# A graph layer on one core: edge blocks of the rounds two to a segment, and four buffers for them

## The chip, the cores and the metric

The kernel runs on one core of one Trainium2 chip. The metric is the device time of one execution in microseconds (us). The profile is of one execution.

## The reference

The layer has N = 6250 nodes with 128 features, and E = 206250 edges with 128 features each, sorted by their target `dst`. What is computed:

```python
h = node_features @ W_node.T + b_node
e = edge_features @ W_edge.T + b_edge
msg = (h[src] + e) @ W_msg.T + b_msg
s = segment_sum(msg, dst)
deg = segment_sum(ones, dst)
out = layernorm(x + s / maximum(deg, 1)[:, None])
```

Since all of it up to the division is linear, the sum over a node's edges can be taken first, once of the edges' features and once of the x of their sources, and the weights applied after.

## The kernel before

Two streams of work are interleaved by a list of slots u = 0 to 135. Slots 0 to 10 (LEAD) are the lead. The 125 others are segments: 25 rounds (ROUNDS, one for each group of 250 nodes) of five segments s = 0 to 4 (SEGS). In the code g = u - LEAD counts segments, m is the round.

**Edge blocks.** The edges come in NS = 101 blocks t of 2048 (1 MB each). SP loads a block into one of EDGE_SLOTS = 3 buffers (`load_edges`, L365); a load waits until TensorE is through with the block that had the buffer (`l1_done`). VectorE makes a one-hot tile for each block (`make_onehot`, L683, ONEHOT_SLOTS = 3 buffers) and a placing matrix (`make_place`, L689, two buffers). TensorE sums the block into windows of 32 nodes (`sum_windows`, L513): 16 fp32 matmuls with 32 columns of weights, which the trace shows as 32 passes. ScalarE copies the windows out of PSUM (`copy_windows`, L1114), TensorE puts them in place (`place_windows`, L520), and VectorE adds the result to `sums_e` at a column that it reads into a register first (`add_sums`, L692 and L699).

**Segments.** Each segment has five fills. A fill is five matmuls that count, from one-hots of rows and keys, how often each source block occurs (`count_fill`, L565, three PSUM banks), and behind it 5 or 6 matmuls of 250 columns that apply the counts of the round before to x (`apply_counts`, L581). ScalarE moves each bank out (`move_bank`, L1167); fill k waits until bank k - 3 is moved. VectorE makes the one-hots for a whole segment ("hots", `make_hots`, L709, two buffers) one segment ahead: those for segment g + 1 may start once TensorE has filled the last bank of segment g - 1. In segment 1 of a round VectorE also makes the keys of the next round (`make_keys`, L723 to L738); TensorE turns them in segment 3 behind fill 2 (`turn_keys`), ScalarE spreads them (`spread_keys`, L1157).

**Finishing.** Group n is finished in segment 0 of round n + 2 on TensorE (`finish_group`, L597, behind fill 3), and in segment 1 on VectorE: message (L748), bias (L755), stats (L762), variance (L770), scale (L775, L777). ScalarE takes the root of the variance in segment 1 between moving banks 2 and 3 (`take_root`, L1179), and normalizes in segment 2 ahead of bank 0 (`normalize`, L1185). SP loads the residual (L384) and stores y (L388) at places in its own order of edge loads.

**Order.** In a segment each engine works in this order. TensorE: the block's sums, fill 0, fill 1, the block's placing, fills 2 to 4. ScalarE: the copy of the block, banks 0 to 4. VectorE: hots of the next segment, message, add_sums, bias, place, stats, one-hot, variance, scale, keys. Before the change a slot has one block or none (`block_at`): one in each slot of the lead, and 90 in segments 1 to 4 of the rounds, all but ten of these. Segment 0 has none.

**Lead.** Beside its 11 blocks the lead finds where each node's edges begin: a window of dst is gathered by POOL (L455), VectorE and ScalarE count in it (L803, L1127), the starts go to DRAM and back (L1132 to L1145), and small gathers fetch src (L463). x (3.2 MB) is loaded behind block 9. In rounds 0 and 1 VectorE also has checks and the splitting of x in three bf16 parts (L873, L879).

Of the kernel before, what the change touches and what calls it, by code (L numbers as in the profile page):

```python
# [27 lines left out]
SEGS = 5  # L28
# [4 lines left out]
G0 = 7  # L33
FIRST = 27
LEAD = 11
EDGE_SLOTS = 3
ONEHOT_SLOTS = 3
COUNT_BANKS = 3
BLOCK = 128
BELOW, ABOVE = 220, 358  # L40
# [4 lines left out]
def gnn_layer(nc, x, src, dst, edge_attr, w_node, b_node, w_edge, b_edge, w_msg, b_msg, out):  # L45
    N = x.shape[0]
    E = edge_attr.shape[0]
    NS = -(-E // SUP)
# [3 lines left out]
    ROUNDS = GROUPS  # L52
# [18 lines left out]
    SLOTS = LEAD + ROUNDS * SEGS  # L71
    group_of = [(G0 + m) % GROUPS for m in range(ROUNDS)]
    sup_of = [(FIRST + t) % NS for t in range(NS)]
    block_at, blocks_by = [], [0]
    for u in range(SLOTS):
        m, s = divmod(u - LEAD, SEGS)
        due = u + 1 if u < LEAD else LEAD + -(-(NS - LEAD) * (m * (SEGS - 1) + s) // (ROUNDS * (SEGS - 1)))
        block_at.append(blocks_by[-1] if due > blocks_by[-1] else None)
        blocks_by.append(due)
    slot_of = [block_at.index(t) for t in range(NS)]  # L80
    assert blocks_by[-1] == NS


    finish_slot = [LEAD + SEGS * (m + 2) if m < ROUNDS - 2 else SLOTS for m in range(ROUNDS)]
    finish_at = {u: m for m, u in enumerate(finish_slot) if u < SLOTS}
    summed_by = [blocks_by[u] for u in finish_slot]
    assert not any(block_at[u] is not None for u in finish_at)

    LIMIT_B = (42.5, 3.6)
    LIMIT_A = (7.3, 3.6)  # L90
# [6 lines left out]
    with ExitStack() as ctx:  # L97
# [385 lines left out]
        def _(pe):  # L483
# [117 lines left out]

            pe.wait_ge(rel_copied, 2)
            for u in range(SLOTS):
                t, g = block_at[u], u - LEAD
                if t is not None:
                    sum_windows(t)
                if u < LEAD:
                    if t == 1:
                        pe.wait_ge(count_taken, 1)
                        count_blocks(1)  # L610
                    if t == 4:
                        turn_weights()
                    if t == 8:
                        turn_slots(0)
                    place_windows(t)
                    if t == 5:
                        make_weights()
                    if t == 9:
                        turn_keys(0)
                    continue  # L620
                m, s = divmod(g, SEGS)
                for f in range(FILLS):
                    count_fill(g, f)
                    if m > 0:
                        apply_counts(m - 1, s * FILLS + f, ROUND_FILLS)
                    if f == 1 and t is not None:
                        place_windows(t)
                    if f == 2 and s == 3 and m + 1 < ROUNDS:
                        turn_keys(m + 1)
                    if f == 3 and u in finish_at:  # L630
                        finish_group(finish_at[u])
                    if f == 3 and g == 2:
                        turn_degrees()
                        turn_slots(1)
# [35 lines left out]
        def _(dve):  # L670
# [9 lines left out]
            def make_onehot(t):  # L680
                if t >= ONEHOT_SLOTS:
                    dve.wait_ge(l1_done, t - ONEHOT_SLOTS + 1)
                dve.tensor_tensor(onehot[:, t % ONEHOT_SLOTS, :, :], iota_bf[:, 0:W].rearrange("p (a w) -> p a w", a=1).to_broadcast([P, TILES, W]),  # L683
                                  rel_col[:, :, sup_of[t]:sup_of[t] + 1].to_broadcast([P, TILES, W]), ALU.is_equal).then_inc(onehot_ready, 1)
# [252 lines left out]
            make_onehot(0)  # L937
            make_place(0)
            make_onehot(1)
            block_counts(1)  # L940

            for u in range(SLOTS):
                t, g = block_at[u], u - LEAD
                n = finish_at.get(u - 1)
                if 0 <= g < SLOTS - LEAD - 1:
                    make_hots(g + 1)
                if n is not None:
                    add_message(n)
                if u < LEAD:
                    if t == 1:  # L950
                        begin_job(1)
                    if 2 <= t < 6:
                        count_nodes(0, [0, 3, 8, 13][t - 2], [3, 8, 13, 18][t - 2])
                    if t == 4:
                        dve.wait_ge(wm_turned, 1)
                        link(dve.tensor_copy(wm_t, x_ps[0][:, 0:D]))
                        dve.wait_ge(small_in, 96)
                        link(dve.tensor_scalar(bias_rep, ones[:, :], bias_col[:, 0:1], bias_col[:, 1:2], ALU.mult, ALU.add))
                        dve.sem_inc(wm_ready, 1)
                    if t == 5:  # L960
                        end_job(0)
                    if t == 6:
                        copy_weights()
                    if t == 7:
                        count_nodes(1, 0, JOB_DVE[1])
                    if t == 8:
                        end_job(1)
                        make_slots(0)
                    if t == 9:
                        make_keys(0)  # L970
                if t is not None:
                    add_sums(t)
                if n is not None:
                    add_bias(n)
                if t is not None and t + 1 < NS:
                    make_place(t + 1)
                if n is not None:
                    take_stats(n)
                if t is not None and t + 2 < NS:
                    make_onehot(t + 2)  # L980
                if n is not None:
                    take_variance(n)
                if u == LEAD - 1:
                    make_hots(0)
                if n is not None:
                    make_scale(n)
                if g >= 0:
                    m, s = divmod(g, SEGS)
                    if s == 1 and m + 1 < ROUNDS:
                        make_keys(m + 1)  # L990
                    if g == 0:
                        make_degrees()
                        check_order()
                    if g == 1:
                        check_sorted()
                    if g == 2:
                        make_slots(1)
                        check_slots()
                        copy_degrees()
                        for i in range(7):  # L1000
                            split_rest(i)
                    if g == 3:
                        for i in range(7):
                            split_low(i)
                        dve.sem_inc(early_done, 1)
                        dve.sem_inc(viol_ready, 1)
# [97 lines left out]
        def _(act):  # L1104
# [86 lines left out]
                act.copy(rel_col[:, k * 8:(k + 1) * 8, :], count_ps[k][:, :].bitcast(BF16).rearrange("p (t c) -> p t c", t=8)[:, :, 0:NS]).then_inc(rel_copied, 1)  # L1191
            roots, ends = 0, 0
            for u in range(SLOTS):
                t, g = block_at[u], u - LEAD
                if g >= 0 and g % SEGS == 0 and g // SEGS >= 2:
                    take_x(g // SEGS - 2)
                if t is not None:
                    copy_windows(t)
                if u < LEAD:
                    k0 = JOB_DVE[0]  # L1200
# [14 lines left out]
                m, s = divmod(g, SEGS)  # L1215
# [59 lines left out]
```

## Time and profile before

| | |
|---|---|
| median of 3 runs | 811.5 us (810.43 to 813.04) |
| the profiled execution | 810.29 us |
| its span, first to last instruction | 808.4 us |
| TensorE busy (matmuls) | 726.8 us, 90% |
| VectorE busy | 636.3 us, 79% |
| ScalarE busy | 461.0 us, 57% |
| GpSimd busy | 49.9 us, 6% |
| moved by DMA | 121.08 MB, 150 GB/s on average |
| chain that ended last | TensorE 85%, VectorE 7%, DMA 4% |

Busy time is the sum over the instructions of an engine. In the rows below L12 is line 12 of the kernel, PE is TensorE, PEld its weight loads, DVE is VectorE, ACT is ScalarE, POOL is GpSimd, and SP issues loads and stores. What stands in square brackets is the idle time of the engine just before the instruction and what ended it; "issue" is a wait for nothing that the profile shows.

### The profile page before, as it was taken

The numbers are of one execution on the slowest core, as the hardware profiler recorded it, in microseconds if no ns is written. First come the engines' busy times: TensorE is split into PE (matmuls) and PEld (weight loads), VectorE is DVE, ScalarE is ACT, GpSimd is POOL, SyncE is SP. The second block draws the span as 40 slices with busy tenths as digits, with TensorE's granted clock in tenths as the row PEclk, the third lists the DMA queues.
The fourth block names the chain that finished last, engine by engine and source line by source line (L and its number), as shares of the span: only waits on it lengthen the run. The fifth ranks groups of instructions, "written<-read, shape, count | busy, mean of one in ns | idle before, by whom it ended". The sixth has DMA issues, their size and how long they took to land.

```text
span 808.4 us, 24794 instructions
## 1 busy us (share of the span) xinstructions
PE 726.8 (90%) x10555; PEld 643.4 (80%) x10555; DVE 636.3 (79%) x1128; ACT 461.0 (57%) x938; POOL 49.9 (6%) x42
## 2 busy tenths in 40 slices
PE   3454636999999999999999999999999999999995
PEld 2333435988898899889889888988888988898895
DVE  6564998798789878888888888878887887788732
ACT  4343632666566566565656665666666656565641
POOL 2002100000000000000000000000000000000000
PEclk9655657999999999999999999999999999999998
DMA  7987431544535444544553465346334544454300
GB/s 223 248 266 232 154 106 54 167 135 155 163 122 177 161 151 138 174 130 137 186 174 119 127 208 168 97 140 221 122 124 156 173 156 128 165 169 134 99 15 15
DMA packets 71529, 121.08 MB, mean 150 GB/s; under 512 B 4486, under 2 KB 17502, under 8 KB 71315
## 3 DMA queue, kind: packets, MB, share of 16 engines
q1 hardware_dynamic: 68462, 115.72, 44.8%
q0 software_dynamic: 2336, 2.83, 1.3%
q8 instruction: 86, 1.41, 0.7%
q10 hardware_dynamic: 618, 0.90, 0.5%
q14 instruction: 27, 0.22, 0.1%
HBM read 116.18 MB, written 3.23 MB: 148 GB/s over the span
## 4 chain that ended last, share of the span: by engine, by line
PE 85%; DVE 7%; DMA 4%; issue 2%; ACT 1%; ACTq 0%; DVEq 0%; POOLq 0%
PE x_ps L581 49%; PE count_ps L565 18%; PE win_ps L513 12%; PE win_ps L520 3%; DMA edges<-in_edge_attr_dram 2%; PE misc_ps L597 1%; PE misc_ps L598 1%; DVE key_hot L709 1%; DVE x_rest L879 1%; DMA win_src<-in_src_dram,clipped_int 1%; DVE row_hot L803 1%; DMA region<-in_dst_dram 1%; DVE row_hot L709 1%; DVE x_rest L873 1%; DMA starts_dram<-edge_total 1%
## 5 line engine op out<-in xcount | busy, mean ns | idle before, releaser
L1167 ACT CAST region<-count_ps 128x490 bf16<-128x490 f32 x625 | 350.2, 574 | 174.1 <-PE count_ps L565 168.0
L581 PE MATMUL x_ps<-region,x_rest 128*128 128x250 bf16 x2450 | 449.3, 270 | 0.0
L581 PE MATMUL x_ps<-region,x_hi 128*128 128x250 bf16 x1225 | 332.6, 271 | 0.0
L709 DVE TENSOR_TENSOR row_hot<-iota_bf,row 125x3200 bf16<-125x3200 bf16 x125 | 227.8, 1822 | 94.6 <-PE count_ps L565 64.3
L565 PE MATMUL count_ps<-key_hot,row_hot 125*128 125x98 bf16 x3125 | 244.2, 209 | 28.3 <-DVE key_hot L709 28.2
L565 PEld LDWEIGHTS count_ps<-key_hot,row_hot 125*128 125x128 bf16 x3125 | 199.8, 99 | 57.0 <-DVE key_hot L709 29.9
L581 PEld LDWEIGHTS x_ps<-region,x_rest 128*128 128x128 bf16 x2450 | 229.6, 98 | 17.4
L709 DVE TENSOR_TENSOR key_hot<-iota_bf,key 125x2500 bf16<-125x2500 bf16 x125 | 181.7, 1454 | 0.0
L513 PE MATMUL win_ps<-edges,onehot 128*32 128x128 f32 x3232 | 118.7, 292 | 11.2 <-DMA edges<-in_edge_attr_dram 9.4
L581 PEld LDWEIGHTS x_ps<-region,x_hi 128*128 128x128 bf16 x1225 | 118.9, 97 | 8.0
L513 PEld LDWEIGHTS win_ps<-edges,onehot 128*32 128x32 f32 x3232 | 89.0, 116 | 32.6 <-issue 21.8
L463 POOL DMA_INDIRECT win_src<-in_src_dram,clipped_int x25 | 44.6, 1785 | 591.1 <-DVE key_bf L738 471.4
L1114 ACT COPY win_sb<-win_ps 128x128 f32<-128x128 f32 x101 | 26.9, 266 | 91.2 <-PE win_ps L513 81.7
L683 DVE TENSOR_TENSOR onehot<-iota_bf,rel_col 128x512 f32<-128x512 bf16 x101 | 68.8, 681 | 0.0
L520 PE MATMUL win_ps<-place,win_sb 128*128 128x128 f32 x202 | 43.9, 301 | 16.2 <-ACT win_sb L1114 13.8
L520 PEld LDWEIGHTS win_ps<-place,win_sb 128*128 128x128 f32 x202 | 32.7, 204 | 21.0 <-ACT win_sb L1114 18.3
L699 DVE TENSOR_TENSOR sums_e<-sums_e,win_ps 128x128 f32 x101 | 28.7, 284 | 15.9 <-PE win_ps L520 9.4
L689 DVE TENSOR_SCALAR place<-iota_f,pos 128x128 f32<-128x128 f32 x101 | 28.7, 284 | 0.1
L1179 ACT ACTIVATE stddev<-mean_var,eps_col 125x2 f32<-125x2 f32 x25 | 7.4, 296 | 35.0 <-DVE mean_var L770 35.0
L1185 ACT ACTIVATE y<-y,shift,rstd 125x128 f32<-125x128 f32 x50 | 22.0, 489 | 0.9 <-DVE shift L777 0.9
L748 DVE SCALAR_TENSOR_TENSOR y<-misc_ps,recip,resid 125x128 f32<-125x128 f32 x50 | 15.1, 343 | 8.9 <-PE misc_ps L598 8.9
L803 DVE TENSOR_SCALAR_CACHE_REDUCE row_hot<-region,job_node 125x578 bf16<-125x578 int32 (+7 forms) x25 | 17.0, 739 | 6.3 <-DMA region<-in_dst_dram,job_idx 6.3
(166 smaller groups left out, 318.6 us busy)
## 6 DMA issues: line engine op xcount, KB each, us to landing
edges<-in_edge_attr_dram SPq DMA_DIRECT2D x101, 1024.0 KB, 5.6
resid<-in_x_dram SPq DMA_DIRECT2D x25, 125.0 KB
out_dram<-y SPq DMA_DIRECT2D x25, 125.0 KB
region<-in_dst_dram ACTq DMA_DIRECT2D x1, 768.0 KB
win_src<-in_src_dram,clipped_int POOLq DMA_INDIRECT x25, 6.6
region<-in_L_gnn_W_node_dram SPq DMA_DIRECT2D x1, 64.0 KB
region<-in_L_gnn_W_edge_dram SPq DMA_DIRECT2D x1, 64.0 KB
region<-in_L_gnn_W_msg_dram SPq DMA_DIRECT2D x1, 64.0 KB
```

The lines of the kernel that those rows point to most:

```text
L463: pool.indirect_dma_start(out=win_src[:, m % 3, :], out_offset=None, in_=src.rearrange("(r e) -> r e", e=WE), in_offset=bass.IndirectOffse ...
L513: mm = pe.matmul(bank[q * W:(q + 1) * W, 0:D], hot[:, q * J + j, :], edges[:, t % EDGE_SLOTS, q * J + j, :], start=(j == 0), stop=(j == J ...
L520: pe.matmul(l2_ps[t % 2], win_sb[:, t % 2, :], place[:, t % 2, :], start=True, stop=True).then_inc(l2_done, 1)
L565: mm = pe.matmul(count_ps[fill % COUNT_BANKS][:, k * KEYS:(k + 1) * KEYS], row_hot[0:WE, g % 2, f * FILL + k, :], key_hot[0:WE, g % 2, f * ...
L581: mm = pe.matmul(x_ps[m % 2][:, 0:NB], rows, counts[m % 2][:, b, :], start=(n == 0), stop=(n == PARTS - 1))
L683: dve.tensor_tensor(onehot[:, t % ONEHOT_SLOTS, :, :], iota_bf[:, 0:W].rearrange("p (a w) -> p a w", a=1).to_broadcast([P, TILES, W]), rel ...
L689: dve.tensor_scalar(place[:, t % 2, :], iota_f[:, :], pos[:, sup_of[t]:sup_of[t] + 1], None, ALU.is_equal).then_inc(place_ready, 1)
L699: dve.tensor_tensor(to, to, l2_ps[t % 2], ALU.add).then_inc(added, 1)
L709: ins = dve.tensor_tensor(hot[0:WE, g % 2, :, :].rearrange("p w (a b) -> p w a b", b=4), iota_bf[0:WE, 0:width].rearrange("p (c a b) -> p ...
L803: dve.tensor_scalar(dve_junk[nodes[0] % 2][0:PB, 0:hi - lo], win_of[k][0:PB, lo:hi], job_node[k][:, i:i + 1], None, ALU.is_lt, ALU.add, ac ...
L1114: act.copy(win_sb[:, t % 2, :], win_ps[t % 2][:, 0:D]).then_inc(win_copied, 1)
L1167: act.copy(counts[m % 2][:, :, f * FILL * 2:(f + 1) * FILL * 2], count_ps[fill % COUNT_BANKS][:, 0:FILL * KEYS].rearrange("p (n b) -> p b ...
```

## The change

The blocks of the rounds are given out in pairs: 45 segments have two, the others none. `blocks_at` lists the blocks of each slot; the due time counts pairs. The lead keeps one block a slot. Edge buffers and one-hot buffers are four in place of three. TensorE sums both blocks at the segment's start and places both behind fill 1; ScalarE copies both at the start; VectorE adds both, then makes two places and up to two one-hots. Places and one-hots are counted by `placed` and `hot`: places run up to two ahead of the slot's last block, one-hots up to three ahead of its first.

```diff
-EDGE_SLOTS = 3
-ONEHOT_SLOTS = 3
+EDGE_SLOTS = 4
+ONEHOT_SLOTS = 4
...
-    block_at, blocks_by = [], [0]
+    blocks_at, blocks_by = [], [0]
     for u in range(SLOTS):
         m, s = divmod(u - LEAD, SEGS)
-        due = u + 1 if u < LEAD else LEAD + -(-(NS - LEAD) * (m * (SEGS - 1) + s) // (ROUNDS * (SEGS - 1)))
-        block_at.append(blocks_by[-1] if due > blocks_by[-1] else None)
+        pairs = -(-((NS - LEAD) // 2) * (m * (SEGS - 1) + s) // (ROUNDS * (SEGS - 1)))
+        due = u + 1 if u < LEAD else LEAD + 2 * pairs
+        blocks_at.append(list(range(blocks_by[-1], due)))
         blocks_by.append(due)
...
             for u in range(SLOTS):
-                t, g = block_at[u], u - LEAD
-                if t is not None:
+                g = u - LEAD
+                for t in blocks_at[u]:
                     sum_windows(t)
...
-                    if f == 1 and t is not None:
+                    for t in blocks_at[u] if f == 1 else []:
                         place_windows(t)
...
             make_onehot(1)
+            placed, hot = [1], [2]
             block_counts(1)
...
-                t, g = block_at[u], u - LEAD
+                ts, g = blocks_at[u], u - LEAD
+                t = ts[0] if ts else None
...
-                if t is not None:
+                for t in ts:
                     add_sums(t)
                 if n is not None:
                     add_bias(n)
-                if t is not None and t + 1 < NS:
-                    make_place(t + 1)
+                while ts and placed[0] < min(NS, ts[-1] + 1 + (1 if u < LEAD - 1 else 2)):
+                    make_place(placed[0])
+                    placed[0] += 1
                 if n is not None:
                     take_stats(n)
-                if t is not None and t + 2 < NS:
-                    make_onehot(t + 2)
+                while ts and hot[0] < min(NS, ts[0] + ONEHOT_SLOTS):
+                    make_onehot(hot[0])
+                    hot[0] += 1
...
-                if t is not None:
+                for t in blocks_at[u]:
                     copy_windows(t)
```

## Rows read from the trace of the kernel before

**Rows 1.** Table of stretches: busy us (instructions) by engine, clock, DMA share, GB/s.
```profile
160.00:780.00 620.00, 620.00 (x9222) 554.78 (x9220) 512.12 (x833) 387.39 (x788) 35.56 (x19) 1.00 0.46 148
```

**Rows 2.** Waits of the run: who for whom, us in total, times, longest.
```profile
PE count_ps L565 <- DVE key_hot L709: 28.2, 5, 9.5
...
PE win_ps L513 <- DMA edges<-in_edge_attr_dram: 9.4, 2, 9.1
```

**Rows 3.** The waits of TensorE's weight loads from 160 us on.
```profile
PEld win_ps L513 <- issue: 16.9, 82, 0.2
```

**Rows 4.** Timeline, TensorE at a block: start us, us, engine, line [idle before].
```profile
406.43 0.27 PE L581 MATMUL x_ps<-region,x_rest 128*128 128x250 bf16 x1
...
406.63 1.08 PE L513 MATMUL win_ps<-edges,onehot 128*32 128x128 f32 x32
407.64 0.25 PEld L565 LDWEIGHTS count_ps<-key_hot,row_hot 125*128 125x128 bf16 x5 [0.20 <-issue]
```

**Rows 5.** Chain that ended last, a fill and a placing: start us, us, what.
```profile
136.78 0.22 PE count_ps L565 x5
137.00 0.64 PE x_ps L581 x6
137.65 0.23 PE win_ps L520 x2
```

**Rows 6.** The timeline, the sum behind that placing.
```profile
138.01 0.29 DVE L699 TENSOR_TENSOR sums_e<-sums_e,win_ps 128x128 f32 x1 [0.63 <-PE win_ps L520]
```

**Rows 7.** Timeline, VectorE in the finishing segment that begins at 406.54.
```profile
409.92 0.29 DVE L699 TENSOR_TENSOR sums_e<-sums_e,win_ps 128x128 f32 x1
...
410.65 0.28 DVE L689 TENSOR_SCALAR place<-iota_f,pos 128x128 f32<-128x128 f32 x1
...
411.24 0.68 DVE L683 TENSOR_TENSOR onehot<-iota_bf,rel_col 128x512 f32<-128x512 bf16 x1
411.83 0.24 DVE L770 BATCH_NORM_AGGREGATE mean_var<-stats 125x2 f32<-125x6 f32 x2
...
414.04 1.82 DVE L709 TENSOR_TENSOR row_hot<-iota_bf,row 125x3200 bf16<-125x3200 bf16 x1
```

**Rows 8.** Timeline, VectorE in the lead: a sum and the instruction ahead.
```profile
76.19 0.29 DVE L738 SCALAR_TENSOR_TENSOR key_bf<-past,src_block 125x125 bf16<-125x125 bf16 x1
77.00 0.29 DVE L699 TENSOR_TENSOR sums_e<-sums_e,win_ps 128x128 f32 x1 [0.52 <-issue]
```

**Rows 9.** The timeline, ScalarE's casts and TensorE's fill 1 of the next segment.
```profile
410.04 0.57 ACT L1167 CAST region<-count_ps 128x490 bf16<-128x490 f32 x1 [0.52 <-PE count_ps L565]
...
412.31 1.02 ACT L1167 CAST region<-count_ps 128x490 bf16<-128x490 f32 x2
...
414.10 0.39 PE L565 MATMUL count_ps<-key_hot,row_hot 125*128 125x98 bf16 x5
```

**Rows 10.** Timeline, round 0: from a segment's one-hots to its first count.
```profile
113.13 1.81 DVE L709 TENSOR_TENSOR row_hot<-iota_bf,row 125x3200 bf16<-125x3200 bf16 x1
...
116.37 0.83 PE L565 MATMUL count_ps<-key_hot,row_hot 125*128 125x98 bf16 x8 [9.50 <-DVE key_hot L709]
```

**Rows 11.** The table of stretches, 2 us each, in the lead.
```profile
16.00:18.00 2.00, 1.22 (x24) 1.25 (x28) 2.00 (x4) 0.00 (x0) 0.00 (x0) 1.00 0.31 54
24.00:26.00 2.00, 0.46 (x2) 0.30 (x2) 1.07 (x3) 0.00 (x0) 1.20 (x1) 1.00 1.08 230
```

**Rows 12.** The chain that ended last, the load of block 3.
```profile
18.76 15.29 DMA edges<-in_edge_attr_dram
```

**Rows 13.** The timeline, VectorE's sums of block 3.
```profile
37.43 0.29 DVE L699 TENSOR_TENSOR sums_e<-sums_e,win_ps 128x128 f32 x1
```

**Rows 14.** Gathers of dst (L455): duration ns, first and last start us, landing.
```profile
L455 POOL DMA_INDIRECT region<-in_dst_dram,job_idx x2: 1196/1324/1452, 14.2 to 24.2; - x2
...
DMA to landing us min/median/max: 12.9/15.0/17.1
```

**Rows 15.** The small gathers of src (L463) up to 100 us: landing.
```profile
DMA to landing us min/median/max: 3.1/5.8/7.1
```

More of the change, by code:

```diff
@@ L73, in gnn_layer @@
     sup_of = [(FIRST + t) % NS for t in range(NS)]
-    block_at, blocks_by = [], [0]
+    blocks_at, blocks_by = [], [0]
     for u in range(SLOTS):
         m, s = divmod(u - LEAD, SEGS)
-        due = u + 1 if u < LEAD else LEAD + -(-(NS - LEAD) * (m * (SEGS - 1) + s) // (ROUNDS * (SEGS - 1)))
-        block_at.append(blocks_by[-1] if due > blocks_by[-1] else None)
+        pairs = -(-((NS - LEAD) // 2) * (m * (SEGS - 1) + s) // (ROUNDS * (SEGS - 1)))
+        due = u + 1 if u < LEAD else LEAD + 2 * pairs
+        blocks_at.append(list(range(blocks_by[-1], due)))
         blocks_by.append(due)
-    slot_of = [block_at.index(t) for t in range(NS)]
-    assert blocks_by[-1] == NS
+    slot_of = [next(u for u in range(SLOTS) if t in blocks_at[u]) for t in range(NS)]
+    assert blocks_by[-1] == NS and max(len(ts) for ts in blocks_at) <= 2
     finish_slot = [LEAD + SEGS * (m + 2) if m < ROUNDS - 2 else SLOTS for m in range(ROUNDS)]
@@ L86, in gnn_layer @@
     summed_by = [blocks_by[u] for u in finish_slot]
-    assert not any(block_at[u] is not None for u in finish_at)
+    assert not any(blocks_at[u] for u in finish_at)
     LIMIT_B = (42.5, 3.6)
@@ L1193, in _ @@
             for u in range(SLOTS):
-                t, g = block_at[u], u - LEAD
+                g = u - LEAD
                 if g >= 0 and g % SEGS == 0 and g // SEGS >= 2:
                     take_x(g // SEGS - 2)
-                if t is not None:
+                for t in blocks_at[u]:
                     copy_windows(t)
```

## The prediction

> **What bounds the kernel now.** I read the table of stretches first. From 160 to 780 us TensorE is busy in every microsecond at full clock, VectorE for 512 of the 620 and ScalarE for 387 [rows 1]. So in the rounds each microsecond of TensorE's queue is one of the kernel's, and the other two engines have room on average, though perhaps not at every place. The waits of the whole run come next. TensorE's long ones, 28.2 us in five for one-hots of VectorE and 9.1 us once for an edge block [rows 2], all lie in the lead and in round 0, where VectorE splits x. Then the weight loads from 160 us on: they never wait for an engine worth the name, but 82 times for "issue" ahead of L513, 16.9 us in all [rows 3], and as much again behind each block ahead of L565 [rows 4]. That is once on either side of every edge block, and it is what the change can halve. Last I read one finishing segment instruction by instruction, to see how late VectorE and ScalarE may be there.
>
> **Part 1, the blocks on TensorE: a saving.** Last matmul of a fill at 406.43, next due 0.11 later (six take 0.64 us [rows 5]), so segment 1 of this round begins at T = 406.54. The first L513 starts at 406.63, 0.09 late. The 32 passes take 1.08 us and the last lasts 0.27 us like the wide one ahead of it [rows 4], so they start (1.08 - 0.27) / 31 = 0.026 us apart and the 33rd would start at 407.46. The first L565 starts at 407.64, 0.18 late [rows 4]. A block alone costs 1.10 us, of which 0.27 is the two borders; a second block right behind costs 0.83 if the border between two equal shapes is free. I take it as free, since the four waits ahead of it (one-hots, copy, sums, edges) are all on things long done. Saving: 45 pairs x 0.27 = 12.15 us. If only the border behind the block is saved: 45 x 0.18 = 8.1; if a second block pays all that a first pays, nothing. The placing matmuls L520 take 0.23 us each [rows 5], run between full-width ones and have no such border: 202 before and after, no change.
>
> The Trainium skill (TensorEngine Tiling (Array Packing), Tiling Modes, Key Properties) says "Changing tiling mode (not just tile) drains the TensorE". Its page TensorE: Matmul & The Clock Gate, Part 2, puts the drain at about 128 cycles, 0.053 us at 2.4 GHz, so two borders would be 0.11 us and 45 of them an estimated 4.8 us in place of 12.15. The rows show 0.09 and 0.18; the duration in the trace goes before the page's figure.
>
> **Part 2, the finishing segment on VectorE: a cost.** Counting the new schedule out, pairs fall on segments (1,3), (1,3), (1,4), (2,4), (2) of five rounds, five times over. Group n is finished in segment 1 of rounds 2 to 24, so a pair meets the finishing in 13 rounds: 8 of the kind (1,3) and 5 of the kind (1,4). VectorE's order there is: one-hots of the next segment, message (L748), sums of the blocks (L699), bias, places, stats, one-hots of the blocks, variance (L770), scale, keys, then the hots of the segment after. All times now from T [rows 7]. Before: sums at 3.38, variance ready at 5.53 (L770 starts at 411.83, two in 0.24), next hots at 7.50.
> With the pair:
> - The first placing comes after both blocks and two fills of 0.87 us (136.78 to 137.65 [rows 5]): 1.93 + 1.74 + 0.23 = 3.90. A sum follows its placing by 0.13 us (L520 from 137.65 for 0.23 [rows 5], L699 at 138.01, which waited for it [rows 6]): 4.03. That is 0.65 later than 3.38.
> - The second sum reads its column offset into a register first. Where VectorE's sequencer can't run ahead of the sum, this shows: L738 issued at 76.19 and L699 at 77.00, 0.81 us [rows 8]. Here the sequencer stands at the wait of the first sum until 4.03, so it can't read ahead: +0.81. The near bound is a sum's own 0.29 plus some 0.05 for its semaphore: +0.34. I take 0.81, as the row is of the same instruction in the same position.
> - A second place: it and two stats take 0.59 (410.65 to 411.24), a third of that is 0.19. A second one-hot takes 0.59 (411.24 to 411.83) [rows 7].
> Sum 0.65 + 0.81 + 0.19 + 0.59 = 2.24 us (bounds 1.77 and 2.3).
>
> **Who waits for that.** ScalarE takes the root of the variance between moving bank 2 and bank 3 of this segment. Before, it cast bank 3 at 412.31, 0.24 behind the variance, and 0.57 later (a cast alone, 410.04), at T + 6.34, the bank was free; TensorE wants it for fill 1 of the next segment, at 414.10 = T + 7.56 [rows 9]. Slack 1.22. With the pair in segment 1 and none in segment 2 TensorE comes there at 1.93 + 0.46 + 4.28 + 0.87 = 7.54 (a segment without a block is five times 0.22 and 29.4 matmuls of 0.108, or 4.28) and the bank is free at 6.34 + 2.24 = 8.58. TensorE stands still for 1.04 us, in 13 rounds: 13.5 us.
> Then the hots of segment 3. From the start of row_hot to the first L565 that uses it 3.24 us pass (113.13 to 116.37 [rows 10]), so they are there at 7.50 + 2.24 + 3.24 = 12.98. TensorE leaves segment 2 at 6.67 + 4.28 + 1.04 = 11.99. In the kind (1,3) it has 1.93 us of blocks to do first: no wait, 0.9 us to spare. In the kind (1,4) it has none: 0.99 us more, 5 times, 5.0 us. Together 18.5 us. With the near bound of the second sum the first stall is 0.57 and the second unchanged: 7.4 + 5.0 = 12.4. Above, some 0.1 us a round for the normalizing that ScalarE has also to do: 20.
> Elsewhere VectorE has time: in segments 3 and 4 it runs ahead and its sums wait for nothing, so the second costs 0.34, and a pair 2.2 us in a segment of 6.67. The next hots (of segment 0) wait for the keys, as before, and come 0.7 us ahead of TensorE in the round with one pair, the tightest.
>
> **Part 3, round 0 and the lead: small, uncertain.** In round 0 VectorE is the bound [rows 2]. Ahead of the hots that release round 1 it now makes one more sum and two more places (the one-hots are as many; the extra one of the lead lies in an idle stretch): 0.2 + 2 x 0.19 = +0.6 us.
> The fourth buffer lets load 3 leave right behind the small loads; before, it left at 18.76 and landed at 34.05 [rows 12]. The DMA engines were 0.31 busy from 16 to 18 us and 1.08 from 24 to 26 [rows 11]. TensorE's 9.1 us there go. But VectorE, counting, comes to the sums of that block only at 37.43, and then waits for nothing [rows 13], so this gain I cost at nothing. The counting itself starts when the window of dst lands, 17.1 us after its issue at 14.2 [rows 14]. That window (124 rows of 1650 words, 0.82 MB) had the engines nearly to itself from 16 to 20 us, at 54 GB/s and more: 0.3 MB. The other 0.52 MB took the 11.3 us to 31.3, 46 GB/s. With load 3 beside it those 0.3 MB take 6.5 us in place of 4: 2.5 us later, and all behind it with it. Bounds 0 and +3. Load of x and blocks 10 to 12 also leave a block earlier, so the first small gather of src (68 us) meets a shorter queue; such gathers landed in 3.1 to 7.1 us [rows 15]. I take 1.0 off, bounds 0 and 4.0. Together +1.5, between -4 and +3.
> SP's queue: x, the residuals and the stores stand behind a load that is released a block earlier. A store behind the second load of a pair waits for its y until some 10 us into the round, and delays an edge load that has 15 us left. Nothing.
>
> **The sum.** -12.15 + 18.5 + 0.6 + 1.5 = +8.5 us. The profiled execution took 810.3 us (span 808.4 and 1.9 around it), the median of the three runs is 811.5. So 818.8 by the one and 820.0 by the other; I say 819.
>
> **The rivals.**
> A, VectorE's lateness is covered (faster). On average VectorE has room, 108 of 620 us [rows 1]. If the variance comes less than 1.22 us later (that is the point at which it decides, at the first L770 of a paired segment 1), only the borders count: 810.3 - 12.15 + 2.1 = 800.3. Against it: 0.65 + 0.19 + 0.59 alone, with a second sum for nothing, is 1.43. Chance 0.15.
> B, the second sum is cheap (0.34): -12.15 + 12.4 + 2.1 = +2.4, 812.7. Against it stands the 0.81 of [rows 8]. Chance 0.15, half of it within the bound of no change.
> C, the change doesn't do what it says: the second block pays its borders too. TensorE then comes 0.27 later to the bank, the stalls are 13 x 0.77 + 5.0 = 15.0, and with 2.1 that is +17.1, 827. Against it: five matmuls of one shape in a row show no border anywhere, only L513's neighbours do [rows 3, 4]. Chance 0.12, which also covers that only a part of the 0.27 is saved.
> By the Trainium skill's figure of the drain, above, the time would be an estimated 826, next to C.
> Forecast: 0.58.
>
> **How the numbers follow.** The forecast's own range goes from 814 (lead -4) to 824 (8.1 us of saving, stalls of 20). The range of 8 in 10 takes in B and C and leaves A out: 806 to 828, the low end being B with the lead's best. About 0.3% (2.4 us) is what a measurement of this kernel can tell from no change. Faster by more: A and the low end of B, 0.17. Within: 0.10. Slower: 0.73.
>
> **What would show it.** Right: issue waits ahead of L513's loads from 160 us on down from 82 to about 41; a second L513 block 0.83 us behind the first; about 13 waits of TensorE or its weight loads at the count for ScalarE's cast, 1 us each, and 5 for key_hot; VectorE idle 0.5 us between two sums in segment 1. Wrong: no waits of TensorE after 160 us (A), or issue waits still 82 or more (C). The lead shows in when the window lands (31.3 before).

## The result and the profile after

The kernel with the change takes 830.16 us (median of four runs, 829.68 to 831.59). The kernel before, beside it on the same chip, takes 810.96 (810.39 to 813.04). The ratio is 1.0218, with a 95% interval of 1.0186 to 1.0249: slower by some 19 us. The forecast was 819.0 with a range of 806 to 828, so the result lies outside it. The sign was as forecast, and so was the mechanism in the rounds; the size was under half, +8 us where +19 came, and the lead lost by a path that the forecast did not have. The profiled executions span 808.4 us before and 827.9 us after, 19.5 us more; the rest of the text accounts for these 19.5.

First the waits of TensorE's weight loads and matmuls from 160 us on, in the kernel after. The columns are: who waited at which line, for whom, us in total, times, longest.

```profile
PEld count_ps L566 <- ACT region L1172: 19.1, 13, 1.8
PEld win_ps L514 <- issue: 8.4, 41, 0.2
PEld count_ps L566 <- issue: 8.1, 41, 0.2
PEld count_ps L566 <- DVE key_hot L710: 5.3, 6, 1.0
```
```profile
PE count_ps L566 <- ACT region L1172: 15.5, 13, 1.5
PE count_ps L566 <- DVE key_hot L710: 3.6, 5, 0.7
```

The issue waits ahead of L514 (L513 before) went from 82 to 41 [rows 3]. Thirteen waits for ScalarE's cast and five for key_hot are new, in exactly the numbers counted out of the schedule. The table of stretches shows the same from TensorE's side. The columns are us, then busy us (instructions) of PE, PEld, DVE, ACT and POOL, the clock, the DMA share and GB/s.

```profile
160.00:780.00 620.00, 600.88 (x9028) 547.06 (x9026) 511.85 (x818) 376.82 (x775) 35.54 (x19) 1.00 0.44 146
```

TensorE was busy in all of the 620 us [rows 1]; now it is idle for 19.1, which is the 15.5 and 3.6 of its own waits above. VectorE's busy time is unchanged, 512 us.

The finishing segment answers [rows 4], [rows 7] and [rows 9]. Here is the timeline of the same segment of the same round. TensorE's two blocks and the count behind them come first, then the last matmul of fill 0 of the segment after, and the late count of fill 1:

```profile
418.54 0.27 PE L582 MATMUL x_ps<-region,x_rest 128*128 128x250 bf16 x1
418.74 1.95 PE L514 MATMUL win_ps<-edges,onehot 128*32 128x128 f32 x64
420.62 0.40 PE L566 MATMUL count_ps<-key_hot,row_hot 125*128 125x98 bf16 x5
...
426.07 0.27 PE L582 MATMUL x_ps<-region,x_hi 128*128 128x250 bf16 x1
427.51 0.40 PE L566 MATMUL count_ps<-key_hot,row_hot 125*128 125x98 bf16 x5 [1.17 <-ACT region L1172]
```

VectorE and ScalarE in between:

```profile
422.90 0.29 DVE L700 TENSOR_TENSOR sums_e<-sums_e,win_ps 128x128 f32 x1 [0.98 <-PE win_ps L521]
423.72 0.29 DVE L700 TENSOR_TENSOR sums_e<-sums_e,win_ps 128x128 f32 x1 [0.53 <-DVE sums_e L700]
423.92 0.61 DVE L756 SCALAR_TENSOR_TENSOR y<-bias_row,has_edge,y 125x128 f32<-125x128 f32 x2
424.44 0.48 DVE L690 TENSOR_SCALAR place<-iota_f,pos 128x128 f32<-128x128 f32 x2
...
425.24 1.27 DVE L684 TENSOR_TENSOR onehot<-iota_bf,rel_col 128x512 f32<-128x512 bf16 x2
426.43 0.24 DVE L771 BATCH_NORM_AGGREGATE mean_var<-stats 125x2 f32<-125x6 f32 x2
```
```profile
426.70 0.29 ACT L1184 ACTIVATE stddev<-mean_var,eps_col 125x2 f32<-125x2 f32 x1 [2.89 <-DVE mean_var L771]
426.90 1.02 ACT L1172 CAST region<-count_ps 128x490 bf16<-128x490 f32 x2
```

The segment begins at T = 418.65 (418.54 and 0.11). The first sum is at T + 4.25, the second 0.82 later, the variance starts at T + 7.78 (before: 411.83 - 406.54 = 5.29 [rows 7]). ScalarE stands 2.89 us at the root with a filled bank behind it. TensorE was due to go on at 426.18 (426.07 and 0.11, T + 7.53) and does so at 427.51: 1.33 us of stall. (The row says 1.17 idle, as it counts the matmul ahead as busy for 0.27 us and not for 0.11; the 0.16 have to be added to each idle time to get the stall.) Twelve of the thirteen are like this one. The other, at 317.19, is 1.67 us, where the second sum came 1.17 behind the first.

Five times TensorE also waits for the hots, at the first count of segment 3 in the kind (1,4). The first of the five:

```profile
181.56 0.27 PE L582 MATMUL x_ps<-region,x_hi 128*128 128x250 bf16 x1
182.55 0.40 PE L566 MATMUL count_ps<-key_hot,row_hot 125*128 125x98 bf16 x5 [0.71 <-DVE key_hot L710]
```

It was due at 181.67 (181.56 and 0.11) and is 0.88 us late, as are the four others. The stalls are thus 12 x 1.33 + 1.67 = 17.6 us and 5 x 0.88 = 4.4 us.

In the lead, two things moved. VectorE's first count of the dst window, which began at 31.34 before:

```profile
34.75 0.58 DVE L804 TENSOR_SCALAR_CACHE_REDUCE row_hot<-region,job_node 125x358 bf16<-125x358 int32 x1 [9.62 <-DMA region<-in_dst_dram,job_idx]
```

And the write of the starts to HBM (L1139), whose completion lets ScalarE fetch them back (L1145), after and then before:

```profile
52.89 0.32 ACTq L1139 DMA_DIRECT2D starts_dram<-edge_total  x1
61.29 0.27 ACTq L1145 DMA_DIRECT2D region<-starts_dram  x1
```
```profile
49.57 0.39 ACTq L1134 DMA_DIRECT2D starts_dram<-edge_total  x1
54.61 0.27 ACTq L1140 DMA_DIRECT2D region<-starts_dram  x1
```

Issue to fetch is 8.4 us after and 5.0 before. What lies between is x: its load leaves SP's queue at 45.36 after and at 49.72 before, so after, the write goes out into its traffic.

```profile
45.36 0.87 SPq L379 DMA_DIRECT2D x_rest<-in_x_dram  x1
46.27 11.28 SPq L380 DMA_DIRECT2D x_rest<-in_x_dram  x1
```
```profile
49.72 0.86 SPq L378 DMA_DIRECT2D x_rest<-in_x_dram  x1
```

The table of stretches at the write, before and then after, has the DMA engines 0.02 busy (8 GB/s) and 1.06 busy (293 GB/s):

```profile
48.00:50.00 2.00, 1.07 (x21) 0.58 (x12) 1.66 (x12) 0.00 (x0) 0.00 (x0) 0.50 0.02 8
```
```profile
52.00:54.00 2.00, 0.08 (x4) 0.00 (x0) 1.01 (x10) 0.00 (x0) 0.00 (x0) 1.00 1.06 293
```

To split the run into lead and rounds I use two landmarks that exist in every version: the sixth row_hot, which releases round 1 (124.57 before, 132.23 after), and the rest of the span behind it (683.8 and 695.7). So of the 19.5 us, 7.7 are in the lead and round 0, and 11.9 in the rounds. Over the seven profiles of kernels with single blocks the rest is 682.7 to 684.1 us, so a difference of a few us in it is clear. The split has one weakness: VectorE has added three blocks of round 0 at the landmark before, four after, and two with pairs in segments 2 and 4, so some 1 us may stand on the wrong side of it.

### The profile page after: what moved, and what is told of

Same layout as the page of the kernel before. It is cut to its first block, busy times and chain, and to the rows that moved or that the text cites. A ratio compares the mean times of both kernels' runs of the same rounds, so it can differ in the third digit from the quotient of the medians.

```text
span 827.9 us, 24794 instructions
## 1 busy us (share of the span) xinstructions
PE 718.7 (87%) x10555; PEld 646.8 (78%) x10555; DVE 642.0 (78%) x1128; ACT 456.8 (55%) x938; POOL 49.9 (6%) x42
## 4 chain that ended last, share of the span: by engine, by line
PE 72%; DVE 16%; DMA 5%; issue 3%; ACT 2%; DVEq 1%; ACTq 0%; POOLq 0%
PE x_ps L582 42%; PE count_ps L566 15%; PE win_ps L514 10%; DMA region<-in_dst_dram,job_idx 3%; DVE onehot L684 2%; PE win_ps L521 2%; DVE row_hot L710 2%; DVE key_hot L710 2%; PE misc_ps L598 1%; PE misc_ps L599 1%; DVE sums_e L700 1%; DVE row_hot L804 1%; DMA starts_dram<-edge_total 1%; DVE y L756 1%; DVE x_rest L880 1%
## 5 line engine op out<-in xcount | busy, mean ns | idle before, releaser
L514 PE MATMUL win_ps<-edges,onehot 128*32 128x128 f32 x3232 | 111.0, 293 | 1.8 <-issue 1.8
L514 PEld LDWEIGHTS win_ps<-edges,onehot 128*32 128x32 f32 x3232 | 93.0, 118 | 14.6 <-issue 12.6
L684 DVE TENSOR_TENSOR onehot<-iota_bf,rel_col 128x512 f32<-128x512 bf16 x101 | 65.4, 683 | 0.0
L521 PE MATMUL win_ps<-place,win_sb 128*128 128x128 f32 x202 | 35.8, 298 | 32.4 <-ACT win_sb L1119 26.7
L521 PEld LDWEIGHTS win_ps<-place,win_sb 128*128 128x128 f32 x202 | 28.8, 202 | 36.4 <-ACT win_sb L1119 30.6
L690 DVE TENSOR_SCALAR place<-iota_f,pos 128x128 f32<-128x128 f32 x101 | 25.0, 285 | 0.0
```

The costliest lines, as they stand in the source:

```text
L514: mm = pe.matmul(bank[q * W:(q + 1) * W, 0:D], hot[:, q * J + j, :], edges[:, t % EDGE_SLOTS, q * J + j, :], start=(j == 0), stop=(j == J ...
L521: pe.matmul(l2_ps[t % 2], win_sb[:, t % 2, :], place[:, t % 2, :], start=True, stop=True).then_inc(l2_done, 1)
L690: dve.tensor_scalar(place[:, t % 2, :], iota_f[:, :], pos[:, sup_of[t]:sup_of[t] + 1], None, ALU.is_equal).then_inc(place_ready, 1)
```

## The experiments

Two theories stand at the start. One is the prediction's: the rounds lose because the pairs that fall on segment 1 delay the variance, and this has nothing to do with the buffer; the lead loses by the buffer. The rival is that the pairs themselves, or the fourth buffer's traffic, make the rounds slower everywhere.

Every kernel below computes the whole output. "Before" and "after" are the two kernels; ratios are to the kernel before, measured beside each. "Lead" is the time of the sixth row_hot, "rest" the span behind it.

**The buffer alone.** The kernel before with

```diff
-EDGE_SLOTS = 3
+EDGE_SLOTS = 4
```

> The kernel before with a fourth edge buffer and nothing else. Theory (two places: the buffer costs the lead, the pairs cost the rounds): the window of dst lands some 3.4 us later and the starts come back some 3.3 us later, as in the changed kernel; 810.3 + 6.7 = 817. Rival (the rounds carry all 19.5 us, the lead's shift has another cause in the schedule): 810 to 811.

816.88 us against 813.53, ratio 1.0047 (1.003 to 1.0065). Lead 132.82, rest 682.8. The rounds are untouched (683.8 before), and the whole cost is in the lead: VectorE starts counting at 37.05 and the starts take 8.6 us from write to fetch (55.20 to 63.76). The wait of 9.1 us for load 3 [rows 2] is gone, and nothing came of it. The 817 expected was met in the number only: it was 810.3 and 6.7, and the kernel before took 813.53 here, so the buffer cost 3.4 us by the medians, half of that. The profiled execution of the kernel before, with 810.3, had the shortest gather of dst of all with three buffers and no load held for it, as the table at the end of this section shows.

**The pairs alone.** The kernel after with `EDGE_SLOTS = 3` (its one-hot buffers stay at four).

> The changed kernel with three edge buffers; one-hots stay at four. Theory: the lead is that of before, the rounds those of the changed kernel (13 bank stalls of 1.3 us, 5 hots stalls of 1 us, borders -10.3): 830.2 - 6.7 = 823.5. Rival: 830. If instead the pairs need the fourth buffer, TensorE waits for edges in the rounds and it is over 830.

825.06 us, ratio 1.016 (1.0129 to 1.0191). Lead 126.23, rest 695.3 (after: 695.7). The row of waits for the cast is that of the kernel after to the digit, and so is the one for key_hot:

```profile
PEld count_ps L566 <- ACT region L1172: 19.1, 13, 1.8
...
PEld count_ps L566 <- DVE key_hot L710: 5.3, 6, 1.0
```

So buffer and pairs act in different places: the pairs cost the rounds 11.5 us, the buffer costs the lead. Their timed costs, 1.6% and 0.5%, add up to the 2.2% of the change within the intervals.

**Pairs away from the finishing segment.** The kernel of the pairs alone, with its pairs only in segments 2 and 4 of a round:

```diff
-        pairs = -(-((NS - LEAD) // 2) * (m * (SEGS - 1) + s) // (ROUNDS * (SEGS - 1)))
+        pairs = -(-((NS - LEAD) // 2) * (m * 2 + s // 2) // (ROUNDS * 2))
```

> The run with three edge buffers, but the 45 pairs on segments 2 and 4 alone, so that none meets the finishing in segment 1. Theory (the collision is the rounds' whole cost): no waits of TensorE for casts or hots after 160 us, 823.5 - 22.4 = 801, which is 10 us under the kernel before (the borders). Rival (a pair itself is dear wherever it stands, since VectorE and ScalarE are late behind every pair): 815 to 823.

800.89 us (800.05 to 801.66), ratio 0.9852 (0.9829 to 0.9875). Lead 125.40, rest 672.8: 11.0 us less than before. This is the run that decides. It has as many pairs, as many second sums and as many doubled places as the one above and takes 24 us less (825.06 and 800.89), so a pair is not dear in itself; it is dear in the finishing segment. The 801 expected, and no waits for casts or hots but the one that was there before, were met. The waits from 160 us on and the stretch:

```profile
PEld win_ps L514 <- issue: 8.4, 41, 0.2
PEld count_ps L566 <- issue: 8.1, 41, 0.2
...
PEld count_ps L566 <- DVE key_hot L710: 0.3, 1, 0.3
```
```profile
160.00:780.00 620.00, 619.94 (x9315) 569.34 (x9313) 520.10 (x837) 387.02 (x791) 35.53 (x19) 1.00 0.44 148
```

TensorE is busy throughout again, and does more in the same 620 us: 9315 matmuls and not 9222.

**The root behind the last bank.** The pairs alone, with ScalarE's root behind bank 4 of the finishing segment and its normalizing behind bank 1 of the next:

```diff
-                if u - 2 in finish_at:
-                    normalize(ends)
-                    ends += 1
...
-                    if f == 2 and u - 1 in finish_at:
+                    if f == 1 and u - 2 in finish_at:
+                        normalize(ends)
+                        ends += 1
+                    if f == 4 and u - 1 in finish_at:
```

> The run with three edge buffers and pairs as in the change, but ScalarE takes the root behind bank 4 of segment 1 and normalizes behind bank 1 of segment 2, so that no bank stands behind the variance. Theory (the bank is what TensorE waits for first, the hots of segment 3 second): the 13 cast waits go, the hots waits grow as TensorE comes 1.3 us sooner, 5 x 2.3 + 8 x 0.3 = 13.9 in place of 22.4 us, so 815. Rival (VectorE's lateness alone is the cost and the order on ScalarE doesn't matter): 823.5.

819.18 us (815.69 to 821.57), ratio 1.0063 (1.0041 to 1.0086). The rest is 688.4, 6.9 less than with the pairs alone. The waits for the cast are gone, and those for the hots have grown:

```profile
PEld count_ps L566 <- DVE key_hot L710: 16.3, 14, 2.7
```

That shows the first stall's chain: with the root out of the casts' way the same late variance costs TensorE nothing at the bank. But TensorE then comes 1.3 us sooner to the hots of segment 3, which are as late as before, and waits there, one segment on:

```profile
PE count_ps L566 <- DVE key_hot L710: 12.5, 13, 2.4
```

In the five rounds of the kind (1,4) the idle time there is 2.1 to 2.4 us where it was 0.7, and the eight others are small (at most 0.6). TensorE's idle time from 160 us on goes from 19.1 us (15.5 and 3.6, as in the kernel after) to 12.5. The expectation had this pattern, and 8.5 us less in all; the rest is 6.9 less, the medians 5.9. The 6.9 us are a third of the 22.5 by which the rest exceeds that with no pairs in the finishing segment (695.3 and 672.8).

**The column offsets read ahead.** The pairs alone, with the offsets of both sums read into registers ahead of the first sum:

```diff
-                for t in ts:
-                    add_sums(t)
+                for t, at in zip(ts, [sums_at(t) for t in ts]):
+                    add_sums(t, at)
```

> Pairs as in the change, three edge buffers, but VectorE reads the column offsets of both sums ahead of the first sum. Theory (the 0.82 us between the two sums is the register read behind a wait): the second sum follows 0.35 us behind the first, the 13 cast stalls shrink by 0.47 us each to 0.86, the hots stalls stay as both sides move alike: -6.1 us against the run with three edge buffers (ratio to the kernel before 1.016 there, 1.008 to 1.009 here). Rival (the gap is the second sum's wait for the first one's result): no change, 1.016.

823.15 us against 812.59, ratio 1.0148 (1.0115 to 1.018). Lead 130.58, rest 690.6, 4.7 less than with the pairs alone (the lead of this execution was late by its gather, see below). VectorE in the same round, and TensorE's wait:

```profile
418.74 0.29 DVE L702 TENSOR_TENSOR sums_e<-sums_e,win_ps 128x128 f32 x1 [0.98 <-PE win_ps L521]
419.24 0.29 DVE L702 TENSOR_TENSOR sums_e<-sums_e,win_ps 128x128 f32 x1 [0.21 <-DVE sums_e L702]
```
```profile
PEld count_ps L566 <- ACT region L1174: 14.5, 13, 1.1
```

The second sum is 0.50 us behind the first in place of 0.82. So the register read behind the wait is 0.32 us of it; the sum's own 0.29 and an idle 0.21 for its wait on the sum ahead remain. 13 x 0.32 = 4.2 us follows for the stalls, and 4.6 are measured (19.1 to 14.5). The expectation was 0.35 us between the sums and 6.1 us less: it took the whole gap but the sum itself for the register read, and the wait for the first sum, which it had as the rival, is a part of it too. The timed ratios of the two kernels, 1.0148 and 1.016, can't be told apart by their intervals; the gain is read from the rest and the waits.

**Load of x later.** The kernel with four buffers, and x loaded behind block 10 and not block 9:

```diff
-                if t == 9:
+                if t == 10:
                     load_x()
```

> The kernel before with four edge buffers, but x loaded behind block 10 instead of block 9, so that it leaves after about the same block's sums as before. Theory (x in flight makes the write of the starts late): the write lands 5.0 to 5.5 us behind its issue in place of 8.6, the window of dst lands as late as with four buffers: some 3 us less than with four buffers alone. Rival (the greater depth of edge loads does it): 8 us and more, the time stays.

815.63 us, ratio 1.0042 (1.0026 to 1.0059). Lead 130.34, rest 684.1. The write of the starts now goes out just ahead of x (54.83), and its fetch follows in 5.3 us, as in the kernel before:

```profile
54.79 0.32 ACTq L1134 DMA_DIRECT2D starts_dram<-edge_total  x1
60.07 0.27 ACTq L1140 DMA_DIRECT2D region<-starts_dram  x1
```

So the load of x is the cause of the slow write. Of the 3.3 us that this gives back the lead keeps 2.5 (132.82 to 130.34): VectorE began counting 0.4 us earlier here (36.65 and 37.05), and its wait for the first small gather of src is 1.2 us longer (6.0 and 4.8). The timed ratio moves by 0.0005 only, less than its interval, where some 3 us less were expected: the write's cost is read from the traces, and no timing shows it.

**Load 3 held.** The kernel with four buffers, in which load 3 waits until block 0 is summed, as with three buffers:

```diff
+                elif t == 3:
+                    sp.wait_ge(l1_done, 1)
```

> The kernel before with four edge buffers, but load 3 held until block 0 is summed, as with three. Theory (load 3 beside the gather of dst makes that late): the gather lands about 17 us behind its issue as before, at most 1 us more since load 4 now leaves with load 3; the write of the starts still takes 8.6 us; some 3 us less than with four buffers alone. Rival (the loads behind block 3 do it): the gather takes 21 us or more as with four buffers.

815.45 us, ratio 1.0035 (1.002 to 1.0049). Lead 131.54, rest 683.7. The write of the starts took 8.35 us, as expected with x early. But the gather of dst took 21.5 us and not the 17 that this hold should have brought back, and the time is not clear of that of four buffers alone (1.0047). Here loads 3 and 4 leave together once block 0 is summed, so the edge loads beside the gather are still one more than with three buffers.

**Four buffers, pairs away from the finishing segment.** The kernel after, with only the line of the pairs changed as above.

> The changed kernel with four edge buffers and one line altered: the pairs on segments 2 and 4 alone. Theory: the rounds lose their 22 us of stalls, the lead keeps its 4 to 6 us: ratio to the kernel before 0.985 (as measured with three buffers) + 0.005 to 0.008 = 0.990 to 0.993, near 805. Rival (four buffers are what hurts the pairs): more than that of three buffers by over 1%.

806.03 us (805.43 to 807.0), ratio 0.9929 (0.9904 to 0.9954). Lead 131.26, rest 673.2. The gather took 21.8 us, the starts 8.4. One line of the schedule is worth 0.029 of the time to the kernel after, some 23 us, and by the ratios the fourth buffer costs this version 0.008 against the one with three (0.9852), some 6 us.

**The gather first.** The version with three buffers and pairs in segments 2 and 4, in which SP sends load 3 only when the first dst window has landed:

```diff
+                if t == EDGE_SLOTS:
+                    sp.wait_ge(job_win_in[0], 16)
```

> Three edge buffers, pairs on segments 2 and 4, and SP holds load 3 (and so all behind it) until the first gather of dst has landed. Theory (edge loads beside the gather make it late): alone from 16 us on it moves 54 to 96 GB/s and lands 11 to 15 us behind its issue in place of 17 to 22; block 3 comes late, but VectorE counts meanwhile; 3 to 5 us less than without the hold (ratio to the kernel before 0.985 there, 0.979 to 0.981 here). Rival (the gather is slow by itself): it lands at 17 us or more and the time stays or grows, as the edges come late.

800.78 us against 813.19, ratio 0.9849 (0.9807 to 0.9891): the time of the version without the hold (0.9852), where 3 to 5 us less were expected. Alone, the window lands 13.3 us after its issue and VectorE starts at 27.52, idle only 1.00; but now TensorE stands for block 3:

```profile
27.52 0.59 DVE L806 TENSOR_SCALAR_CACHE_REDUCE row_hot<-region,job_node 125x358 bf16<-125x358 int32 x1 [1.00 <-DMA region<-in_dst_dram,job_idx]
```
```profile
36.60 1.94 PE L516 MATMUL win_ps<-edges,onehot 128*32 128x128 f32 x32 [9.34 <-DMA edges<-in_edge_attr_dram]
```

VectorE has counted by then, and waits for the sum of that block:

```profile
39.85 0.29 DVE L702 TENSOR_TENSOR sums_e<-sums_e,win_ps 128x128 f32 x1 [6.24 <-PE win_ps L523]
```

It began 5.0 us earlier than without the hold (27.52 and 32.49) and stands 6.24 us here; the starts go out at 51.68 us and not at 50.50. That edge loads beside the gather make it late is shown; that its lateness alone costs the run is not.

**The spread of the lead.** The kernel before twice more, and the kernel with four buffers once more:

> The kernel before once more, for the spread of its lead. Theory (with three buffers the gather of dst lands 17 to 22 us behind its issue from run to run, with four always 21 to 23): a landing in 17 to 22, the write of the starts back after 5.0 to 5.7 us. Rival (the gather's time is the buffers' alone): 17.1 again.

> The kernel before a third time: as for the second look, gather in 17 to 22 us, starts in 5.0 to 5.7 us.

> The kernel before with four edge buffers once more. Theory: the gather lands 21 to 23 us behind its issue, the write of the starts is back after 8.3 to 8.7 us. Rival (both vary at random): values down to 17 and 5.

| | us | gather of dst | write to fetch of starts | lead |
|---|---|---|---|---|
| before again | 813.08 | 20.6 | 5.3 | 128.26 |
| before, third | 809.77 | 17.8 | 5.3 | 125.18 |
| four buffers again | 819.37 | 21.7 | 8.6 | 133.39 |

The gather of the kernel before thus took 17.1 us [rows 14] to 20.6, and its lead came out up to 3.7 us apart (124.57 to 128.26). With three buffers it took 17.1, 17.4, 18.4, 21.1, 21.9, 20.6 and 17.8 us (mean 19.2), with four 21.1, 22.7, 22.5, 21.5 (load 3 held), 21.8 and 21.7 (mean 21.9). By the means the fourth buffer costs 2.7 us there; the pair of profiles shows more, as 17.1 is the shortest of these. From 24 to 32 us the DMA engines are full in all of them (a share of 1.04 to 1.06), and where the window was early they moved more: 251 GB/s with 17.1 us, 245 with 17.8, 206 with 20.6. The write of the starts doesn't vary: 4.9 to 5.7 us with three buffers, 8.4 to 8.6 with four, 5.3 with four and x later. VectorE's wait for the first small gather of src is 5.4 to 7.0 us with three (mean 5.8) and 4.8 to 5.9 with four and x early (mean 5.2).

## Why the prediction was right in sign and short in size

| term of the sum | forecast | measured | how |
|---|---|---|---|
| borders | -12.15 | -10.3 to -11.0 | 45 x 0.23; rest of the run with pairs in segments 2 and 4 |
| stalls at the cast | +13.5 | +17.6 | 12 x 1.33 and 1.67 |
| stalls at the hots | +5.0 | +4.4 | 5 x 0.88 |
| round 0 | +0.6 | +0.9 | first hots +6.8, releasing hots +7.7 |
| gather of dst | +2.5 | +3.4 | 31.34 to 34.75 (by the means over all profiles +2.7) |
| first small gather of src | -1.0 | -0.1 | VectorE's idle time ahead of it, 5.67 to 5.54 (by the means -0.6) |
| write of the starts | 0 | +3.4 | 5.0 to 8.4 |

With -10.3 the measured terms come to +19.3, beside 19.5 in the spans. The forecast's come to +8.5. Of the 10.8 between them the stalls at the cast are 4.1, the write of the starts 3.4, the borders 1.9, and the terms of the two gathers 1.8.

**What held.** What bounds the kernel (TensorE's queue in the rounds), the count of 13 and 5 waits, the lines at which they appear, the second sum 0.81 behind the first (0.82), the second place (0.20) and second one-hot (0.60), and the hots as the next late thing in the kind (1,4). Rival A, that nothing is late, had its condition wrong for this schedule; moving the pairs out of segment 1 makes it true. That the version with three buffers then takes 800.9, beside the 800.3 of the rival, is luck: the rival counted from 810.3 with a fourth buffer at 2.1 us. It made the change 1.2% faster, and the version with four buffers and the pairs moved is 0.7% faster, since the borders give 10.3 and not 12.15 and the lead costs more. Rival B is refuted by the 0.82. Rival C, that the second block pays its borders too, is refuted by the 41 waits in place of 82, and only 0.04 us of the 0.27 isn't saved.

**The second block cost 0.87, not 0.83.** From the first L514 at 418.74 to the count at 420.62 are 1.88 us, where one block takes 1.01 (406.63 to 407.64 [rows 4]). The forecast was 1.10 for a block with its borders, so 0.23 is saved in a pair. The 64 passes start (1.95 - 0.27) / 63 = 0.0267 us apart and not 0.026, which is 0.02 of the 0.04; the rest isn't explained. The Trainium skill (TensorEngine Tiling (Array Packing), Key Properties) has a drain of TensorE at a change of tiling mode. The trace fits that, with a delay on either side of the changed shape and none between equal shapes, but doesn't show that the delay is this drain. The estimate of 4.8 us from the drain of about 128 cycles (the Trainium skill, TensorE: Matmul & The Clock Gate, Part 2) was less than half of the measured saving.

**The step that failed in the rounds: the time of the first sum.** The stall was put at 1.04 and is 1.33. The first sum came at T + 4.25 and not at 4.03. Of these 0.22, 0.05 is the second block and the two fills (the placing starts at 422.37, T + 3.72, and not at 3.67). The rest is in "A sum follows its placing by 0.13 us (L520 from 137.65 for 0.23 [rows 5], L699 at 138.01...)". This took the placing's start from the chain and put it behind fills timed in the timeline. The two views date the same instruction differently. The chain says 137.65, where its predecessor's modelled end is. The timeline of the kernel before says:

```profile
137.49 0.39 PE L520 MATMUL win_ps<-place,win_sb 128*128 128x128 f32 x2
```

From there the sum follows by 0.52 and not by 0.36, and the missing 0.16 us reappears as lateness. At a place with a slack of 1.22, each error in the lateness goes into the stall undiminished, 13 times: 13 x 0.22 = 2.9 of the 4.1 us. The rest are the 0.34 of the one longer stall, 0.03 in the steps up to the variance, which is 2.49 late in all and not 2.24 (7.78 - 5.29), and 0.04 from the end of the cast (426.90 and 0.57) to the matmul at 427.51, which the forecast left out.

**The step that failed in the lead: what x is moved past.** "Load of x and blocks 10 to 12 also leave a block earlier, so the first small gather of src (68 us) meets a shorter queue" was costed as a gain alone, by the gather that comes behind. What comes beside x wasn't looked up: ScalarE's write of the starts, at 49.57 us just ahead of x before, is at 52.89 us in the midst of it after. That is 3.4 us on the path of round 0. The gain of 1.0 was 0.1 in this pair of profiles and 0.6 by the means over all. The part of the prediction on SP's queue listed x, the residuals and the stores, all of which stand in that queue; the loser stands in ScalarE's queue, and what it shares with x are the DMA engines, 1.06 busy at its time. The experiment with x later confirms this cause of the slow write. The range left 4 us for a better lead and only 3 for a worse one.

**Still open.** Why load 3 held back (21.5 us) didn't bring the gather to 17 can't be told from its spread, which reaches 21.9 us with three buffers. The buffer's timed cost is shown, 0.35 to 0.47% with single blocks and 0.8% with pairs in segments 2 and 4 (0.9929 and 0.9852); with the pairs of the change it is 0.6% (1.0218 and 1.016), and there the intervals touch. How it is shared between gather and write is so in this pair of profiles only: neither share is timed alone.

## What to carry to other kernels

Read the slack of every place where the moved work lands, not the engine's free share: VectorE had 108 us to spare in 620, and 1.22 us at the place that counted, and as many pairs are worth -1.5% or +1.6% by the segment they are put in. When an in-order engine does a short dependent step between moves that free another engine's banks, whatever feeds that step is on the bank's path. When a load is released earlier, list what shares the DMA engines with it at its new time, on every queue, not only what stands behind it in its own.

## What the runs showed of the hardware

- A block of 32 passes of 128x32 f32 weights among matmuls with full-width bf16 weights cost 0.23 us at its borders that a second such block right behind didn't pay again; the second took 0.87 us for 32 passes.
- A sum whose column offset is read into a register behind a wait started 0.82 us behind the sum ahead, and with the offset read before, 0.50: 0.29 of work and 0.21 idle for one VectorE instruction that waits for another.
- A small write to HBM took 4.9 to 5.7 us until the fetch behind it could go when it was sent within 1 us of the load of x (3.2 MB), and 8.4 to 8.6 when it was sent 6 to 8 us behind that load, into its traffic.
- A gather of 0.82 MB landed in 13.3 us with the DMA engines a quarter busy (0.25 from 18 to 28 us), in 17.1 to 21.9 us with the edge loads of three buffers beside it, and in 21.1 to 22.7 with those of four. The two ranges overlap, and the seven and six profiles differ by 2.7 us in the mean. Between profiled executions of the kernel before it differed by 3.5 us.
